# A two-layer graph network: layer two's sums computed transposed, in five stretches of 500 source nodes

## The reference

```
h = relu(layernorm(x))
x = x + segment_sum((h @ W0)[src] * edge_weight[:, None], dst)        # layer one
h = relu(layernorm(x))
row = concat(src, arange(N)); col = concat(dst, arange(N))            # self loops
deg = count of row;  norm = deg[row]**-0.5 * deg[col]**-0.5
x = x + segment_sum(norm[:, None] * (h @ W1.T + b)[col], row)         # layer two
```

## Time and profile before

| | |
|---|---|
| median of three runs | 1748.61 us (1748.29 to 1752.34) |
| the profiled execution | 1750.08 us |
| its span (first to last instruction) | 1748.3 us |
| TensorE busy | 1554.0 us (89%), 8627 matmuls |
| VectorE busy | 930.2 us (53%) |
| ScalarE busy | 456.5 us (26%) |
| GpSimd busy | 556.2 us (32%) |
| mean granted TensorE clock | 0.966 |

### The profile page before, as it was taken

One profiled execution on the slowest core, in us unless ns is written; L12 is line 12 of the kernel. 1 busy time (PEld: TensorE's weight loads), 2 busy tenths in 40 slices (PEclk: granted clock), 3 DMA queues, 4 the chain that ended last, 5 costly groups with the idle time before them and its releaser, 6 DMA issues.

```text
span 1748.3 us, 30157 instructions
## 1 busy us (share of the span) xinstructions
PE 1554.0 (89%) x8627; PEld 792.7 (45%) x8628; DVE 930.2 (53%) x1747; ACT 456.5 (26%) x783; POOL 556.2 (32%) x1494
## 2 busy tenths in 40 slices
PE   2566699995979999999998999979999999999998
PEld 1233355543545454444554545334444444444443
DVE  6956556425977678777776776382313131313121
ACT  2514454531212222222222222271212121212110
POOL 0112444213656677677676774000000000000000
PEclk9977899997989999999999999999999999999999
DMA  7201242107546565666565666671232323232310
GB/s 262 97 1 32 64 139 61 29 16 165 114 97 141 125 142 135 144 145 139 133 151 129 146 140 150 201 230 55 63 99 66 96 66 96 66 96 66 96 37 25
DMA packets 449659, 185.86 MB, mean 106 GB/s; under 512 B 376677, under 2 KB 431993, under 8 KB 449544
## 3 DMA queue, kind: packets, MB, share of 16 engines
q1 hardware_dynamic: 449544, 184.63, 41.5%
HBM read 77.06 MB, written 77.11 MB: 88 GB/s over the span
## 4 chain that ended last, share of the span: by engine, by line
PE 54%; DVE 14%; issue 11%; POOLq 5%; POOL 5%; DMA 4%; SPq 4%; DVEq 2%; ACT 2%; ACTq 0%
PE pair L1392 19%; PE pair L1304 12%; PE pair L1253 9%; PE pair L1316 7%; PE pair L1265 5%; POOLq L522 3%; POOL fbuf L525 2%; SPq L357 2%; POOL fbuf L527 2%; DVE slots L774 2%; DMA a_scratch<-area 2%; DVE slots L775 2%; DVE h L939 1%; PE pair L1422 1%; SPq L378 1%
## 5 line engine op out<-in xcount | busy, mean ns | idle before, releaser
L1316 PE MATMUL pair<-h,area 128*128 128x512 f16 x2400 | 551.0, 383 | 2.6 <-issue 1.9
L1316 PEld LDWEIGHTS pair<-h,area 128*128 128x128 f16 x2400 | 234.2, 99 | 265.5 <-issue 18.2
L1265 PE MATMUL pair<-slots 128*128 128x240 f16 x1624 | 209.3, 275 | 104.8 <-DVE slots L775 54.6
L525 POOL CAST fbuf<-etab 128x12 f16 (+1 forms) x640 | 192.9, 301 | 152.4 <-DVE slots L775 79.2
L1048 ACT ACTIVATE area<-pair 128x320 f32<-128x320 f32 x160 | 69.9, 437 | 643.2 <-PE pair L1265 439.9
L1265 PEld LDWEIGHTS pair<-slots 128*128 128x128 f16 x1624 | 157.3, 100 | 171.4 <-issue 73.0
L979 DVE SCALAR_TENSOR_TENSOR agg_s<-pair,sc,agg_s 128x512 f16<-128x512 f32 x40 | 28.2, 747 | 350.7 <-ACT agg_s L1172 350.7
L1304 PE MATMUL pair<-wmat,agg_t 128*128 128x512 f16 x960 | 210.4, 379 | 1.6 <-ACT agg_t L1179 1.6
L527 POOL TENSOR_TENSOR fbuf<-etab,negbase 128x4 f16 (+2 forms) x640 | 200.9, 314 | 0.0
L1392 PE MATMUL pair<-h,etab 128*128 128x512 f16 x800 | 182.1, 379 | 8.9 <-DVE h L939 8.7
L1392 PE MATMUL pair<-h,slots 128*128 128x512 f16 x800 | 180.5, 379 | 0.0
(11 more groups left out here) (181 smaller groups left out, 1316.1 us busy)
## 6 DMA issues: line engine op xcount, KB each, us to landing
c_scratch<-area SPq DMA_DIRECT2D x160, 160.0 KB, 2.2
a_scratch<-area SPq DMA_DIRECT2D x320, 80.0 KB, 2.2
area<-c_scratch SPq DMA_DIRECT2D x20, 1280.0 KB, 7.3
xt<-in_x SPq DMA_DIRECT2D x19, 512.0 KB, 3.6
x_scratch<-xt SPq DMA_DIRECT2D x19, 512.0 KB, 2.9
xt<-x_scratch SPq DMA_DIRECT2D x19, 512.0 KB, 3.6
out_x<-xt SPq DMA_DIRECT2D x19, 512.0 KB, 2.6
h<-x_scratch SPq DMA_DIRECT2D x4, 2048.0 KB, 10.5
```

The source lines that it names most:

```text
L525: pool.tensor_copy(fbuf[:, s, 1:F, at].rearrange("p f u d -> p u f d"), twice(etab_c[:, bass.ds(c, u), 1:F], [P, u, F - 1, 2])).then_inc(s ...
L1265: return pe.matmul(dest, touches[:, t, 0:P], touches[:, t, P:CS], start=first, stop=last, skip_group_check=True)
L1316: last = pe.matmul(sum_pair(e)[:, half * H:(half + 1) * H], wts(e)[:, q, k, :], hpart(k, r)[:, half * H:(half + 1) * H], start=k == q == r ...
```

## The change

Layer two computes the sums transposed. h is now the weights and the counts are the moving operand, 500 source nodes at a time (NCK = 5 stretches of CW = 500; 5 x 500 = 2500 exactly, so no padding on the source side). Each of the eight feature slices f of a stretch is one PSUM bank [128 features x 500 sources], 20 x 2 matmuls deep. The result has the features on partitions, as the product with W1 wants it as weights: the transposes and the copy after them go. Output tiles have RW = 125 rows, four to a stretch (BPC), and their PSUM pairs alternate between WIN and WO. The second-half matmuls stay behind the same branch, which is now taken once for each f.

The two-column matmuls go. Instead VectorE accumulates the counts times deg**-0.5 over the 20 tiles, both halves (`norms`, 40 instructions a stretch on 128 x 500, each waiting for the last), into `s_acc`, and four f32 matmuls of one column sum it over partitions. For rows by 125, degrees are loaded a second time (`deg_u`) and transposed a second time.

Counts are loaded as ten pairs of tiles a stretch (128 x 2 x 500, 512 KB, 2000 B runs), into a ring of two slots in the first stretch and four later; a slot is loaded again when `ct_lo` says that its pair was converted. The diagonal is added by GpSimd. First halves lie in one buffer of 20 x 500, remainders in `etab` and `slots`.

In the first stretch the sums run over source tiles k as h comes: k 0 to 3 for four slices, then for the other four, then k 4 to 15 for all eight, then the last four tiles slice by slice. Later stretches run slice by slice over three banks. VectorE's and ScalarE's orders around the passage change with it: pairs 0 to 5 are converted in layer one's end, 6 to 9 between the scales and the splits.

```diff
@@ SyncE
+            def load_counts(c, j):
+                use = landed(c, j)
+                if use > 1:
+                    before = max(NPC * b + i + 1 for b in range(c + 1) for i in range(NPC)
+                                 if ring_of(b, i) == ring_of(c, j) and NPC * b + i < NPC * c + j)
+                    sp.wait_ge(ct_lo, before)
+                elif c > 0:
+                    sp.wait_ge(h2_ready, T)
...
             sp.wait_ge(win_sum, NQ)
-            load_counts(1, 1)
+            for j in range(4):
+                load_counts(0, j)
             sp.wait_ge(degrow_ready, 1)
             sp.dma_start(deg_dram, deg_row).then_inc(deg_out, 16)
             sp.wait_ge(deg_out, 16)
...
+            for j in range(4, 6):
+                load_counts(0, j)
             store_x1(last, 0)
...
             for k in range(4):
                 sp.wait_ge(sup_free, k + 1)
                 load_x1(k)
+                load_counts(0, 6 + k)
...
+            for j in range(4):
+                load_counts(1, j)
+            for c in range(NCK):
+                for b in range(BPC):
+                    m = BPC * c + b
+                    if c + 1 < NCK:
+                        for j in {0: (4, 5, 6, 7), 1: (8, 9)}.get(b, ()):
+                            load_counts(c + 1, j)
+                        if c + 2 < NCK and b == BPC - 1:
+                            for j in range(4):
+                                load_counts(c + 2, j)
+                    store_tile(m)
+                    if m + 2 < T:
+                        load_rows(m + 2)
@@ VectorE
+            for j in range(2):
+                counts_left(0, j)
             dve.wait_ge(deg_sum, 1)
             nc.vector.tensor_reduce(deg_row, WIN[0:KB, 0:SW].rearrange("p (w n) -> p n w", w=4), AX.X,
                                     ALU.add).then_inc(degrow_ready, 1)
+            for j in range(2, 4):
+                counts_left(0, j)
+            dve.wait_ge(deg_tp, 2)
...
             variances(0, T - 1)
-            self_loops(0, 0)
+            counts_left(0, 6)
             dve.wait_ge(std_ready, 8)
             chain(nc.vector.reciprocal(dinv[:], dinv[:]))
             scales(0, T - 1)
...
+            counts_left(0, 7)
+            split(0)
...
+            for t in range(1, 3):
+                split(t)
+            counts_left(0, 8)
+            residual(T // 2 - 1, 1)
+            moments_of_x1(T // 2 - 1, 1)
+            split(3)
+            counts_left(0, 9)
...
+            for c in range(NCK):
+                step = T // KD + 1
+                if c == 0:
+                    norms(c, 0, T)
+                for f in range(KD):
+                    sums2_left(c, f)
+                    if c > 0:
+                        norms(c, min(T, step * f), min(T, step * (f + 1))) if step * f < T else None
+                for b in range(BPC):
+                    if c + 1 < NCK:
+                        for j in {0: range(8), 1: range(8, NPC)}.get(b, ()):
+                            counts_left(c + 1, j)
+                    finish(BPC * c + b)
@@ ScalarE
+            for j in range(6):
+                counts_first(0, j)
             act.wait_ge(var_ready, 7)
...
+            for j in range(6, 8):
+                counts_first(0, j)
             act.wait_ge(norm_ready, 7)
...
+            for c in range(NCK):
+                for f in range(KD):
+                    act.wait_ge(agg2_ready, KD * c + f + 1)
+                    act.activation(agg_of(f, 0), sums_of(c, f), ACT.Copy, scale=sc[:, 15:16]).then_inc(aggs2_ready, 1)
+                if c + 1 < NCK:
+                    act.wait_ge(acc_ready, c + 1)
+                    for j in range(NPC):
+                        counts_first(c + 1, j)
@@ TensorE
+            def by_counts(c, f, k, counts, first=False, last=False):
                 for q in range(2):
+                    ins = pe.matmul(sums_of(c, f), hpart(k, q)[:, f * P:(f + 1) * P], counts, start=first and q == 0,
+                                    stop=last and q == 1, skip_group_check=True)
+                return ins
...
+            def products(c):
+                for b in range(BPC):
+                    m = BPC * c + b
+                    need(pe, y_ready, m - 1)
+                    if b == 0:
+                        pe.wait_ge(aggs2_lo, KD * c + 2)
                     for k in range(KD):
+                        if b == 0 and k > 1:
+                            pe.wait_ge(aggs2_lo, KD * c + k + 1)
+                        for q, r in ((0, 0), (0, 1), (1, 0)):
+                            for half in range(2):
+                                last = pe.matmul(out_pair(m)[0:RW, half * H:(half + 1) * H],
+                                                 agg_of(k, q)[:, b * RW:(b + 1) * RW],
+                                                 wmat[:, r, k, half * H:(half + 1) * H], start=k == q == r == 0,
+                                                 stop=k == KD - 1 and q == 1)
+                    last.then_inc(wout2_ready, 1)
+                    if b == 0:
+                        pe.wait_ge(acc_ready, c + 1)
+                        for i in range(BPC):
+                            last = pe.matmul(TP[0:RW, H + m + i:H + m + i + 1], s_acc[:, i * RW:(i + 1) * RW],
+                                             ones[:, 0:1], start=True, stop=True)
+                        last.then_inc(s_summed, 1)
```

More of the change, by code:

```diff
@@ L574, in _, with self_loops @@
                 sum_counts(n, n % 2)
+            def self_loops(c, j):
+                pool.wait_ge(c_landed[ring_of(c, j)], 16 * landed(c, j))
+                for t in range(KT):
+                    d0 = (KT * j + t) * P
+                    a, b = max(d0, c * CW), min(d0 + P, (c + 1) * CW)
+                    if a < b:
+                        own = landing(c, j)[:, t, a - c * CW:b - c * CW]
+                        pool.tensor_tensor(own, own, ident[:, a - d0:b - d0], ALU.add).then_inc(own_done, 1)
+                pool.wait_ge(own_done, sum(diagonals(b, i) for b in range(c + 1) for i in range(NPC if b < c else j + 1)))
+                pool.sem_inc(self_ready, 1)
+            for c in range(NCK):
+                for j in range(NPC):
+                    self_loops(c, j)
         @block.vector
@@ L1383, in _ @@
             most = pe.snap(most_reg, min_val=0, max_val=E + 1)
-            pe.wait_ge(h2_ready, 1)
-            pe.wait_ge(dinv_ready, 1)
-            pe.wait_ge(x1_ready, T - 1)
-            def by_h(lhs, e, h_of, d_of, first=False, last=False):
+            def by_counts(c, f, k, counts, first=False, last=False):
                 for q in range(2):
-                    for half in range(2):
-                        pe.matmul(AGG[:, half * H:(half + 1) * H], lhs, h_of(q)[:, half * H:(half + 1) * H],
-                                  start=first and q == 0, stop=last and q == 1, skip_group_check=True)
-                return pe.matmul(bank[e][:, 0:2], lhs, d_of, start=first, stop=last, skip_group_check=True)
@@ new lines, in sums @@
+            def sums(c):
+                for f in range(KD):
+                    need(pe, aggs2_lo, KD * c + f - 2)
+                    for k in range(T):
+                        if f == k % KT == 0:
+                            pe.wait_ge(ct_lo, NPC * c + k // KT + 1)
+                        last = by_counts(c, f, k, ct_hi_of(k), first=k == 0, last=k == T - 1)
+                        if k == T - 2:
+                            second_halves(c, f)
+                    last.then_inc(agg2_ready, 1)
@@ L1450 @@
+            sums_of_first()
+            pe.wait_ge(w1_in, 32)
+            products(0)
+            for c in range(1, NCK):
+                sums(c)
+                products(c)
 _INS = ['x', 'src', 'dst', 'edge_weight', 'L0_gnn_W', 'L1_gnn_W', 'L1_gnn_b']
```

329 lines of the change are left out of this document (142 added, 187 removed).

## The result

The kernel after the change takes 1761.05 us (median of 4 runs, 1760.34 to 1763.87), the kernel before, timed beside it, 1748.45 (1747.96 to 1752.34). The ratio is 1.007, with a 95% interval of 1.0052 to 1.0089: 0.7% slower, where 1.5% faster was forecast. The profiled execution took 1761.72 us, its span 1759.8.

A forecast was written before the change was run, and what follows sets the result against it. Layer two was taken as bound by TensorE's own instructions. First sums end at 1224.0, products and seam 44.5, four stretches 442.0, three seams 4.5, tail 6.9: span 1721.9, forecast 1722 us, 26.4 us faster; range 1708 to 1736.

The forecast's parts named there:

- The steady part: Layer two without stops: a stretch takes 110.5 us against 116.1 before; five stretches give back 28 us.
- The degree sums: Four one-column f32 matmuls a stretch in layer two: 1.2 to 1.9 us, taken as 1.6.
- The branch: Branch over the second halves in layer two, passed 40 times, not 20: 0.01 us each, 4 us at most.
- The seams: Between layer two's stretches: the fourth product waits for tile 1's finish, 1.5 us idle at each of four, 6 us.
- The passage: Layer one to layer two: degrees late, layer one ends 5.5 us later (ends 2 and 9), first sums end at 1224.
- The sum: Whole kernel: first sums end at 1224.0, last matmul at 1715.0, span 1721.9, time 1722 us.
- tail: From the last matmul to the end of the span: 6.9 us, as before.
- (C): Rival: seams are the bound; 7.3 us to landing makes tile 1's finish 5.5 us late, 22 us: 1738; chance 0.15.
- (E): Rival: all at their far ends, passage +9, seams +18, small matmuls +2, branches +4: 1755 us; chance 0.04.
- (D): Rival: 125-column weights in layer two's products load slower, 0.126 us more per matmul, 121 us: 1843; chance 0.08.
- (B): Rival: the passage costs nothing, hidden by 67.5 us of matmuls, and the seams never show: 1702 us; chance 0.11.
- the multiply-adds: VectorE's 40 a stretch over 500 columns: 28 us, hidden under 67.5 us of sums, 6 us to spare in the first.

The follow-up runs named there:

- tops_early: Changed kernel with rows split, counts ahead, degrees ahead of counts, pairs 4 and 5 later, largest degrees reduced before pair 6: 1703.8 us, ratio 0.9722.
- split_rows: Changed kernel with its 125-row stores of y and loads of its rows made as 112 and 13 rows: 1728.8 us, ratio 0.9884.

## Why the prediction was wrong

**The steady part was right.** Sums 67.62 for 67.5, products 41.44 for 41.4, all full clock. The degree sums cost 0.79 us a stretch for 1.6, which I had taken from matmuls of 125 columns in the earlier trace rows; I was 4 us too high in five. The branch shows no cost.

**The seams are the step that failed.** It says "SP stores tile 0, waits for that store (some 3 us)" and that pairs 8 and 9 "land near 28.5" and the finish of tile 1 "ends near 34.3". Against the end of the sums, pairs 8 and 9 were issued at 25.2 us at the second seam (forecast 23.5: the store took 6.2 us for 3, and 1.5 of the rest was less), landed at 34.3 (9.1 us for 5), and the finish ended at 40.8; TensorE went on at 40.9, 6.6 us after the forecast's 34.3. It was free at 32.1 for 32.8, with the cheaper degree sums: 1.5 + 6.6 + 0.7 = 8.8, as measured. Both sizes came from transfers of 128 rows among others of 128 rows. Here the store has 125, and the counts, 128 rows themselves, are issued behind a load of 125; the plan had everything within 1.5 us of the limit, so each us late was a us of standing TensorE. I also gave the slow clock behind a stop no price at the seams, though the earlier trace rows showed one: 9.4 us.

**The passage came out near, but not by its own steps.** The sums of the first stretch ended at 1225.7 for 1224. Yet the degrees were at 1116.1 for 1112, in a run whose degree sum started 1.4 us later, and layer one ended at 1152.1 for 1147.8; the slow matmuls after the stop cost 2.6, and 2.5 were in the forecast. VectorE's chain was less late: the first h was ready at 1151.7 for 1149.5, and the one for which TensorE stood 3.1 us at 1161.5 for 1159.5. As the later of the two chains sets the end, 2 us came through and not 4.3. The forecast had h as the later at the start of layer two, by 1.7 us; in the run layer one's end was, by 0.4. That so little remained was luck.

**The sum.** Span forecast 1721.9, measured 1759.8, 37.9 more: the first sums +1.7, standing at the seams 34.0 - 6 = +28.0, slow matmuls there +9.4, degree sums -4.0, tail +1.2 (the last store has 125 rows: 6.6 us for 5.5), sums +0.5; what is left, 1.1, is the matmul in flight at each stop and rounding.

**The rivals.** (C), the seams as the bound, was the right mechanism, at 5.5 us a seam; it was sized by the old counts loads (7.3 us) and kept the store at 3, and it came to 8.5 and the slow clock. (E) named nearly the time (1755) by other means: its seams were 18 us, the bulk of it; they were 37 over the forecast. (D) fell, and on the point given against it: a load of 125-column f16 weights takes 141 ns, not 98, and the products still stand 0.2158 us apart. The Trainium skill's factor of two for such a load ("TensorE: Matmul & The Clock Gate", Weight-path perf modes) is 1.4 in this trace. (B) was refuted by the passage too: the first sums would have ended at 1209.8 by it, 15.9 us before they did. The range and (E) count 9 us for the passage on top of the sum, but the text gives 2 and 9 as ends of a term that is 5.5 in the sum, 3.5 to either side; with that (E) is 1750. Either is short of 1761.

Settled by runs: the row count sets the speed of a store (four row counts in one kernel); that and the order on SyncE together make the loss (each alone mended takes off 71 to 100% of the standing at the seams); the multiply-adds are hidden. Open: why the stops at the seams with split rows differ (1.3 to 3.9 us), what tops_early gains, and why the time before the degree sum varies by up to 9 us between these kernels.

## What to carry to other kernels

When a change retiles a kernel, put the new row count of each transfer against the 16 DMA engines (its largest divisor up to 16) before taking a duration from the old one: 125 rows were twice as slow as 120 or 128, and 127 rows eight times. Such a transfer costs nothing as long as nothing due soon is queued behind it; look at what SyncE issues after it waits for it, and issue the loads with the nearest deadline first. And if a plan meets its deadline by 1 or 2 us at each of several seams, then its forecast is not "1.5 us each" but a range that starts there.

## What the runs showed of the hardware

- A store of half a megabyte from SBUF to DRAM took 2.8 us with 128 rows (kernel before) and with 112 + 13 (split_rows), 6.2 with 125 (kernel after), and 22 with 127. In the kernel before, SyncE waited 2.3 us for a store of 128 rows, 2.7 for 120 + 8 and 5.4 for 125 + 3.
- The count loads, of 128 rows, into the two slots that are loaded behind a 125-row load landed after 9.0 and 9.8 us (medians of layer two, kernel after), and after 5.2 and 6.1 when the rows went as 112 and 13 (split_rows).
- After a stop of 7 to 9.5 us TensorE's next 48 matmuls took 12.4 to 13.5 us instead of 10.5; with the rows in two pieces, stops of 1.3 and 1.9 us left them at 10.57, and stops of 2.8 and 3.9 us made 12.26 and 13.45.
- An f32 matmul of one column over 128 x 125 weights cost 0.2 us in place, against 0.47 for one of 125 columns (two instructions each).
